# Four attention stages of a two-layer decoder: the order of the score rows, the row maxima and their followers within a batch, and the engine that splits the node biases

## The chip, the cores and the metric

One core of a Trainium2 chip. The time is that of one launch, in microseconds on the device, median of three runs. TensorE multiplies, VectorE (DVE) and ScalarE (ACT) work on tiles and empty PSUM, GpSimd (POOL) works on tiles in SBUF and issues gathers, SyncE (SP) issues the other transfers. The engines run their own instruction streams and meet at semaphores.

## The reference

Four sequences of 256 positions, 128 channels, 16 heads of width 8. Cut to its stages:

```
x = x + L0_attn(layernorm(x))            # kernelised attention (exp features)
x = x + L0_xattn(layernorm(x), ctx)      # softmax attention over ctx, query rows masked
x = x + L0_ffn(layernorm(x))             # three hard-routed trees (q, k, v), attention over
                                         # their outputs, a fourth tree; 255 nodes with bias each
x = x + L1_attn(layernorm(x))            # causal softmax attention
x = x + L1_xattn(layernorm(x), ctx)      # softmax attention over ctx
x = x + L1_ffn(layernorm(x))             # product-key experts, top 16 of 1024 per head

# a softmax attention, per batch and head:
corr = einsum('bhqd,bhkd->bhqk', qh, kh) * scale
prob = softmax(corr, axis=-1)
hidden = einsum('bhqk,bhkd->bhqd', prob, vh)
```

## The kernel before

Work is numbered by n = 4 * stage + batch. n = 0 to 3 is the kernelised attention. The three softmax attentions are in two runs, `RUNS = [(4, 7), (8, 15)]`: batches 4 to 7 are the cross attention of layer 0; then come the trees (`ffn`); batches 8 to 11 are the causal attention and 12 to 15 the cross attention of layer 1; then come the experts (`peer`).

**A batch of a run.** Queries and keys are split into three bf16 parts by GpSimd (`split(n)`), and SP stacks the parts into `stk[n % 3]` with twelve copies of 64 KB (`place(n)`), so that one matmul with a contraction of 51 gives full-precision scores. For each head, `score_rows(n, h)` computes scores with queries on partitions, in two PSUM banks in turn, and VectorE takes each query's maximum (`row_max(n, h)`). When all 16 heads are through, `max_parts(n)` splits the negated maxima into bf16 parts (five instructions), TensorE turns them (`max_turn(n)`), ScalarE copies them out of PSUM (`evac_mt(n)`), and SP copies them into three rows of the stack (`place_max(n)`). Only then can `score_cols(n, h)` compute the scores again with keys on partitions, already less the maximum, in two other banks. ScalarE exponentiates them (`exps(n, h)`), and `values(n, g)` multiplies the probabilities of four heads with the values and a column of ones.

**The followers.** For batch n - 1: `evac_o`, `turn_out` (eight transposes), `onorm` (division by the sums), `tail_a`, `evac_ot`, `tail_b` (output projection), `resid` (VectorE adds it to `x`). For the batches ahead: `norm(n + 3)` with one `power` on GpSimd, `pre_x` (transposes), `evac_x`, `pre_qk`, `evac_qk`, `pre_v`, `evac_v` for n + 2, and its `split` and `place`.

**The order** is written by hand, by head number h, once for each engine, and each engine goes through its list strictly in order. Within batch n, TensorE does `score_cols(n, h)` for h = 0 to 15, and between them the rows of batch n + 1 by

```
ROWS_AT = [[2 * h, 2 * h + 1] if h < 5 else [h + 5] if h < 11 else [] for h in range(H)]
TURN = 13
```

so two heads' rows at each of h = 0 to 4 and one at each of h = 5 to 10. VectorE follows with the maxima, `max_parts(n + 1)` at h = 11 and `norm(n + 3)` at h = 13, `max_turn(n + 1)` is at 13. `pre_x(n + 2)` stands ahead of h = 0. At the start of a run the rows of its first batch run alone.

**The node biases.** The 4 x 255 biases of the trees are split into three bf16 parts on three partitions of `bias_p`, by `split_bias` on VectorE: nine instructions of 255 columns in each of batches 4 to 7, at h = 8. `tree_logits(0)`, behind batch 7, waits for the last (`bias_ready` 3). GpSimd, once the key maximum of stage 0 is reduced over partitions (`kmax_all`), waits in `power(4)` for VectorE's `norm(4)`.

## Time and profile before

| | us |
|---|---|
| median of three runs | 906.93 (904.53 to 907.21) |
| profiled execution, its own time | 905.02 |
| its span, first to last instruction | 903.3 |
| around the span | 1.7 |
| TensorE busy | 704.9 (78%) |
| VectorE busy | 650.5 (72%) |
| ScalarE busy | 443.3 (49%) |
| GpSimd busy | 262.3 (29%) |

The shares are means over stages with different limits. The runs lie from about 123 to 224 us and from 491 to 662 us of the span; the trees stand between them, the experts behind. Times of trace rows are microseconds from the span's start.

### The profile page before, as it was taken

The page shows a single profiled execution, that of the slowest core. Times are in us where ns is not written, and L with a number is a line of the kernel's source. Part 1 is how long each engine was busy: PE and PEld are TensorE (multiplying, and loading weights), DVE is VectorE, ACT ScalarE, POOL GpSimd, SP SyncE. Part 2 cuts the span into 40 slices and gives each one's busy share as a digit, 9 for nine tenths or more (in the row PEclk, how much of TensorE's full clock was granted, in tenths as well). Part 3 has the DMA queues.
Part 4 walks back from the last instruction along what each step waited for, and adds up shares of the span by engine and source line. Part 5 has one row for each costly group of instructions (what it writes and reads, how often), then busy time and mean ns, then how long its engine had stood idle before and what let it go on. Part 6 is the DMA issues. An engine that isn't in the chain of part 4 may idle for free. (4 is left out here: it accounts for less than half of the span.)

```text
span 903.3 us, 15196 instructions
## 1 busy us (share of the span) xinstructions
PE 704.9 (78%) x5016; PEld 529.8 (59%) x5016; DVE 650.5 (72%) x2828; ACT 443.3 (49%) x1051; POOL 262.3 (29%) x242
## 2 busy tenths in 40 slices
PE   3876977878718989888777588887776957878888
PEld 1436524433318777777675366544455956878888
DVE  5665565565559798986596466665538999999984
ACT  1112004345118877888674255555542555565562
POOL 3110221200143232232141121121003027776783
PEclk9886557798958999999888699999997979999999
DMA  8500052200089978898555343322000000000000
GB/s 251 136 1 2 12 64 39 34 6 2 1 308 354 397 275 339 307 397 319 198 194 146 107 54 48 42 38 39 3 1 1 1 1 1 5 4 4 4 8 7
DMA packets 42679, 93.68 MB, mean 104 GB/s; under 512 B 4050, under 2 KB 30194, under 8 KB 34408
## 3 DMA queue, kind: packets, MB, share of 16 engines
q0 software_dynamic: 9216, 69.47, 20.1%
q1 hardware_dynamic: 33384, 23.23, 13.1%
q8 instruction: 40, 0.66, 0.3%
q14 instruction: 39, 0.32, 0.1%
HBM read 74.42 MB, written 0.52 MB: 83 GB/s over the span
## 5 line engine op out<-in xcount | busy, mean ns | idle before, releaser
L742 ACT ACTIVATE arena<-arena,hact 128x128 f32<-128x128 f32 x512 | 155.0, 388 | 1.0
L565 POOL TENSOR_TENSOR arena<-arena 128x1024 f32<-128x1024 f32 x64 | 121.2, 1912 | 82.6 <-DVE arena L1216 65.2
L644 ACT ACTIVATE arena<-psum 128x512 f32<-128x512 f32 (+1 forms) x192 | 102.4, 562 | 81.2 <-PE psum L1366 80.0
L873 DVE TENSOR_REDUCE rowmax<-psum 128x2 f32<-128x512 f32 x128 | 81.5, 686 | 49.6 <-PE psum L1348 48.6
L1067 DVE CUSTOM_DVE_ANT_0 arena<-arena,fx 128x128 f32<-128x128 f32 x384 | 106.0, 344 | 0.3
L1683 PE MATMUL psum<-arena 128*128 128x128 f32 x688 | 86.8, 284 | 21.4 <-DVE arena L1216 19.2
L1572 PE MATMUL psum<-identf,arena 128*128 128x128 f32 x544 | 75.6, 294 | 27.9 <-ACT arena L742 27.3
L1683 PEld LDWEIGHTS psum<-arena 128*128 128x128 f32 x688 | 82.3, 197 | 25.0 <-DVE arena L1216 12.5
L1572 PE MATMUL psum<-arena,identf 128*128 128x128 f32 x544 | 79.5, 304 | 15.3 <-ACT arena L742 14.6
L795 ACT ACTIVATE psum<-arena,tneg 128x1024 f32<-128x1024 f32 x64 | 71.0, 1111 | 39.8 <-POOL arena L565 14.1
L1572 PEld LDWEIGHTS psum<-identf,arena 128*128 128x128 f32 x544 | 68.6, 203 | 35.1 <-ACT arena L742 24.7
L1572 PEld LDWEIGHTS psum<-arena,identf 128*128 128x128 f32 x544 | 72.3, 212 | 22.6 <-issue 16.2
L1348 PE MATMUL psum<-arena 128*128 128x256 bf16 (+1 forms) x384 | 73.7, 291 | 11.9 <-DVE rowmax L873 8.9
L1366 PE MATMUL psum<-arena 128*128 128x256 bf16 (+1 forms) x384 | 70.7, 275 | 12.0 <-DMA arena<-mt 7.5
L587 ACT ACTIVATE arena<-psum 128x128 f32<-128x128 f32 (+3 forms) x66 | 37.9, 577 | 75.5 <-PE psum L1382 18.2
L1216 DVE SCALAR_TENSOR_TENSOR arena<-arena,vaug,psum 128x1024 f32<-128x1024 f32 x43 | 54.3, 1272 | 4.0 <-PE psum L1683 2.3
L1366 PEld LDWEIGHTS psum<-arena 128*128 128x128 bf16 x384 | 32.6, 100 | 37.4 <-ACT arena L644 13.7
L1348 PEld LDWEIGHTS psum<-arena 128*128 128x128 bf16 x384 | 35.3, 104 | 32.7 <-DVE rowmax L873 25.2
L1382 PE MATMUL psum<-arena,vaug 128*32 128x256 f32 (+1 forms) x768 | 51.1, 386 | 1.9 <-ACT arena L644 1.9
L1683 PE MATMUL psum<-arena,picked 128*128 128x128 f32 x336 | 43.2, 283 | 10.5 <-DVE picked L1216 8.2
L473 POOL TENSOR_TENSOR rstd<-var_e,halves 128x2 f32<-128x2 f32 x16 | 11.2, 703 | 136.3 <-DVE var_e L829 136.3
L1683 PEld LDWEIGHTS psum<-arena,picked 128*128 128x128 f32 x336 | 40.2, 196 | 12.3 <-DVE picked L1216 9.8
(215 smaller groups left out, 1235.3 us busy)
## 6 DMA issues: line engine op xcount, KB each, us to landing
arena<-parts SPq DMA_DIRECT2D x144, 64.0 KB
arena<-zeros SPq DMA_DIRECT2D x6, 1232.0 KB
w_sb<-attn_w SPq DMA_DIRECT2D x1, 768.0 KB, 8.1
x<-x_in SPq DMA_DIRECT2D x1, 512.0 KB, 4.4
fx<-ctx_in SPq DMA_DIRECT2D x1, 512.0 KB, 5.4
picked<-mask_in SPq DMA_DIRECT2D x1, 512.0 KB, 6.9
wq_sb<-peer_wq SPq DMA_DIRECT2D x1, 512.0 KB, 7.1
down_sb<-table_down SPq DMA_DIRECT2D x1, 512.0 KB, 7.8
```

The lines of the kernel that those rows point to most:

```text
L565: nc.gpsimd.tensor_tensor(grid[k % 3].rearrange("p (i j) -> p i j", i=PK), sim[:, t, h, :].unsqueeze(2).to_broadcast([P, PK, PK]), sim[:, ...
L644: nc.scalar.activation(probs[k % (2 * HG)][:, 0:w], bank(2 + k % 2, 0, w), ACT.Exp, scale=float(D) ** -0.5).then_inc(probs_ready, 1)
L742: a = nc.scalar.activation(w, w, ACT.Copy, scale=hact[i % 2][:, l:l + 1])
L795: nc.scalar.activation(psum[:, (4 + 2 * (k % 2)) * BANK:(6 + 2 * (k % 2)) * BANK], grid[k % 3], ACT.Exp, bias=tneg[:, t, h:h + 1]).then_in ...
L873: i = nc.vector.tensor_reduce(rowmax[n % 2][:, :, h], bank(k % 2).rearrange("p (s n) -> p s n", s=SUB), AX.X, ALU.max)
L1067: i = nc.vector.tensor_tensor_reduce(w, w, src, 1.0, r[:, LW * E + l:LW * E + l + 1], ALU.mult, ALU.add, hid[g % 4][:, l:l + 1])
L1216: nc.vector.scalar_tensor_tensor(out=picked[k % 3], in0=grid[k % 3], scalar=top[t][:, h, TOPK - 1:TOPK], in1=psum[:, (4 + 2 * (k % 2)) * B ...
L1348: i = nc.tensor.matmul(o[:, r:r + keys], q[:, s * P:s * P + P], kk[:, 0:keys], start=not causal, stop=True, skip_group_check=causal)
L1366: i = nc.tensor.matmul(bank(2 + k % 2, c * S, c * S + S - q0), kk[:, c * P:c * P + P], q[:, q0:S], start=not causal, stop=True, skip_group ...
L1382: i = nc.tensor.matmul(o, vaug[n % 4][:, c, g * HG + j, :], probs[(k + j) % (2 * HG)][:, c * S:c * S + S - q0], start=(c == 0), stop=(c == ...
L1572: i = nc.tensor.matmul(o, *ab, start=(l == 0), stop=(l == LW and f < 3))
L1683: i = nc.tensor.matmul(psum[:, o:o + P], picked[k % 3][:, c * P:c * P + P], diag[t % 2][:, h, :], start=(h == 0 and c % 4 == 0), stop=(h = ...
```

## The change

The rows of a batch are spread by a table of slots. A slot below zero is a head of the batch before: row 0 of batch n + 2 stands at h = 14 of batch n, rows 1 and 2 at h = 15, the other thirteen at h = 0 to 9 of batch n + 1. At the start of a run the three early rows of the second batch follow the first batch's `max_turn`. `max_parts` stands at h = 9 (it was 11), `max_turn` and `evac_mt` at 12 (13), `norm(n + 3)` at 11 (13). `pre_x`, `pre_qk`, `pre_v` stand behind the columns of heads 0, 1, 3 (ahead of head 0, then 0, 1), the `values` groups at 6, 11, 13 and at head 2 of the next batch (5, 9, 13, 1), `turn_out` and `tail_a` at 4 and 7 (3, 6), with ScalarE's and VectorE's lists to match. `norm(6)` moves behind the first batch's `max_parts`, and GpSimd's `split(5)` ahead of `power(6)`. The node biases are split by GpSimd, all 1020 columns at once, ahead of `power(4)`, in a tile of their own.

```diff
-        nbias_sb, nbias_w = arena2[0:3, 4096:5116], arena2[0:3, 3072:3072 + 510].bitcast(bf16)
+        nbias_sb, nbias_w = arena2[0:3, 4096:5116], sb("nbias_w", [3, 4 * NODES], bf16)[:, :]
...
-        ROWS_AT = [[2 * h, 2 * h + 1] if h < 5 else [h + 5] if h < 11 else [] for h in range(H)]
-        TURN = 13
+        ROW_SLOTS = [-2, -1, -1, 0, 1, 1, 2, 2, 3, 4, 4, 6, 6, 7, 8, 9]
+        EARLY = len([i for i in ROW_SLOTS if i < 0])
+
+        def rows_at(n, h, last):
+
+            return ([(n + 1, j) for j in range(H) if ROW_SLOTS[j] == h and n + 1 <= last]
+                    + [(n + 2, j) for j in range(H) if ROW_SLOTS[j] == h - H and n + 2 <= last])
...
             pool.wait_ge(kmax_all, 1)
+            pool.wait_ge(in_tab, 32)
+            p = bias_p[:, 9 * P:NB]
+            for j in range(3):
+                row = identf[0:3, j:j + 1].to_broadcast([3, 4 * NODES])
+                link(nc.gpsimd.tensor_copy(nbias_w, nbias_sb))
+                if j < 2:
+                    link(nc.gpsimd.tensor_tensor(nbias_sb, nbias_sb, nbias_w, ALU.subtract))
+                link(nc.gpsimd.tensor_tensor(nbias_w if j else p, nbias_w, row, ALU.mult))
+                if j:
+                    link(nc.gpsimd.tensor_tensor(p, p, nbias_w, ALU.add))
+            nc.gpsimd.tensor_copy(nbias_w[:, 0:1], p[:, 0:1]).then_inc(nbias_ready, 1)
             power(B)
             power(B + 1)
             split(B)
+            split(B + 1)
             power(B + 2)
-            split(B + 1)
...
# ScalarE, in run()
-                    if n + 2 <= last:
-                        evac_x(n + 2)
                     for h in range(H):
                         exps(n, h)
-                        if n > first and h == 1:
-                            evac_o(n - 1)
-                        if n + 2 <= last and h == 0:
-                            evac_qk(n + 2)
-                        if n + 2 <= last and h == 1:
-                            evac_v(n + 2)
-                        if h == TURN and n + 1 <= last:
+                        if n + 2 <= last:
+                            if h == 0:
+                                evac_x(n + 2)
+                            elif h == 1:
+                                evac_qk(n + 2)
+                            elif h == 3:
+                                evac_v(n + 2)
+                        if n > first:
+                            if h == 2:
+                                evac_o(n - 1)
+                            elif h == 7:
+                                evac_ot(n - 1)
+                        if h == 12 and n + 1 <= last:
                             evac_mt(n + 1)
-                        if h == 8 and n > first:
-                            evac_ot(n - 1)
...
# VectorE
-            norm(B + 2)
             def run(first, last):
                 for h in range(H):
                     row_max(first, h)
                 max_parts(first)
+                if first == B:
+                    norm(B + 2)
+                for h in range(EARLY):
+                    row_max(first + 1, h)
                 for n in range(first, last + 1):
                     for h in range(H):
-                        if n + 1 <= last:
-                            for hh in ROWS_AT[h]:
-                                row_max(n + 1, hh)
-                        if n > first and h == 5:
-                            onorm(n - 1)
-                        if n > first and h == 11:
-                            resid(n - 1)
-                        if n + 1 <= last and h == TURN - 2:
+                        for m, hh in rows_at(n, h, last):
+                            row_max(m, hh)
+                        if n > first:
+                            if h == 4:
+                                onorm(n - 1)
+                            elif h == 9:
+                                resid(n - 1)
+                        if h == 9 and n + 1 <= last:
                             max_parts(n + 1)
-                        if h == 13 and n + 3 <= last:
+                        if h == 11 and n + 3 <= last:
                             norm(n + 3)
-                        if h == 8 and first == B:
...
-                            split_bias(nc.vector, link, j, j + NODES)
...
# TensorE
                 max_turn(first)
+                for h in range(EARLY):
+                    score_rows(first + 1, h)
                 for n in range(first, last + 1):
-                    if n + 2 <= last:
-                        pre_x(n + 2)
                     for h in range(H):
                         score_cols(n, h)
+                        for m, hh in rows_at(n, h, last):
+                            score_rows(m, hh)
+                        if n + 2 <= last:
+                            if h == 0:
+                                pre_x(n + 2)
+                            elif h == 1:
+                                pre_qk(n + 2)
+                            elif h == 3:
+                                pre_v(n + 2)
+                        if n > first:
+                            if h == 2:
+                                values(n - 1, 3)
+                            elif h == 4:
+                                turn_out(n - 1)
+                            elif h == 7:
+                                tail_a(n - 1)
+                            elif h == 9:
+                                tail_b(n - 1)
+                        if h == 6:
+                            values(n, 0)
+                        elif h == 11:
+                            values(n, 1)
+                        elif h == 13:
+                            values(n, 2)
+                        if h == 12 and n + 1 <= last:
+                            max_turn(n + 1)
...
-                    pe.wait_ge(bias_ready, 3)
+                    pe.wait_ge(nbias_ready, 1)
```

## Rows read from the trace of the kernel before

**Rows 1.** Busy time by stretch: batches 4, 5, 7, 8, 11, 14, 15.

```profile
core 0: us, PE busy (x) PEld busy (x) DVE busy (x) ACT busy (x) POOL busy (x), PEclk, DMA share, GB/s
...
139.60:163.80 24.20, 19.79 (x129) 9.99 (x130) 15.58 (x37) 10.34 (x19) 4.94 (x6) 0.78 0.27 35
163.80:190.40 26.60, 21.61 (x159) 11.86 (x158) 15.10 (x35) 11.67 (x22) 4.25 (x5) 0.85 0.24 32
...
213.70:224.30 10.60, 9.56 (x85) 4.78 (x86) 4.03 (x14) 6.96 (x13) 0.00 (x0) 0.88 0.01 2
...
511.80:531.20 19.40, 17.16 (x157) 11.77 (x158) 11.99 (x44) 9.09 (x20) 4.23 (x5) 0.87 0.34 44
...
571.30:591.30 20.00, 16.64 (x170) 11.11 (x170) 13.93 (x33) 10.27 (x23) 4.22 (x5) 1.00 0.33 43
...
632.00:652.30 20.30, 15.88 (x147) 8.71 (x148) 12.11 (x26) 10.47 (x19) 0.00 (x0) 1.00 0.01 3
652.30:661.70 9.40, 8.37 (x85) 4.67 (x86) 1.01 (x4) 6.62 (x12) 0.00 (x0) 1.00 0.00 0
```

**Rows 2.** Timeline of batch 11: start, us, engine, line, [idle before].

```profile
572.06 0.60 PE L1247 MATMUL psum<-xn_t,w_sb 128*128 128x256 f32 x2
...
575.23 1.02 ACT L587 ACTIVATE arena<-psum 128x1024 f32<-128x1024 f32 x1 [1.12 <-PE psum L1382]
...
575.30 0.60 PE L1348 MATMUL psum<-arena 128*128 128x256 bf16 x4
...
575.72 2.48 DVE L873 TENSOR_REDUCE rowmax<-psum 128x2 f32<-128x512 f32 x4 [0.81 <-PE psum L1348]
...
576.47 0.39 PE L1348 MATMUL psum<-arena 128*128 128x256 bf16 x2 [0.29 <-DVE rowmax L873]
...
577.30 1.05 PE L1306 MATMUL psum<-identf,arena 128*128 128x128 f32 x8
...
585.65 2.01 ACT L644 ACTIVATE arena<-psum 128x384 f32<-128x384 f32 x4 [1.46 <-PE psum L1366]
...
588.14 0.86 PE L1382 MATMUL psum<-arena,vaug 128*32 128x256 f32 x16
```

**Rows 3.** The same timeline at the end of batch 11.

```profile
586.48 0.41 DVE L862 TENSOR_TENSOR x<-psum,x 128x256 f32<-128x256 f32 x1
...
587.91 0.29 PE L1394 MATMUL psum<-identb,mparts 128*48 128x128 bf16 x2 [0.78 <-DVE mparts L887]
...
588.25 0.38 ACT L587 ACTIVATE mt<-psum 48x256 bf16<-48x256 bf16 x1 [0.58 <-PE psum L1394]
...
590.69 0.44 PE L1263 MATMUL psum<-identf,xn 128*128 128x128 f32 x2 [1.04 <-DVE xn L834]
...
591.33 0.39 PE L1366 MATMUL psum<-arena 128*128 128x256 bf16 x2 [0.21 <-DMA arena<-mt]
```

**Rows 4.** SP's timeline: the twelve copies of `place`, batches 9 and 13.

```profile
496.41 12.48 SPq L409 DMA_DIRECT2D arena<-parts  x12
...
574.42 7.91 SPq L409 DMA_DIRECT2D arena<-parts  x12
```

**Rows 5.** VectorE's timeline: a node split of 255 biases, first and last of nine.

```profile
181.12 0.27 DVE L261 CAST arena<-arena 3x255 bf16<-3x255 f32 x1
...
184.10 0.28 DVE L271 TENSOR_TENSOR bias_p<-bias_p,arena 3x255 bf16<-3x255 bf16 x1
```

**Rows 6.** GpSimd: its wait for `norm(4)`, and two lines (min/median/max ns).

```profile
100.54 0.74 POOL L473 TENSOR_TENSOR rstd<-var_e,halves 128x2 f32<-128x2 f32 x1 [23.33 <-DVE var_e L829]
```

```profile
L495 POOL TENSOR_TENSOR resid_f<-qk_f,parts x12: 1151/1156/1161, 108.7 to 614.3; 128x512 f32<-128x512 f32 x12
```

```profile
L565 POOL TENSOR_TENSOR arena<-arena x64: 1905/1911/1957, 685.5 to 887.5; 128x1024 f32<-128x1024 f32 x64
```

**Rows 7.** Timelines of VectorE and GpSimd: the first `key_features`; `norm(6)` beside `split(5)`.

```profile
78.61 0.69 DVE L940 TENSOR_SCALAR arena<-arena 128x1024 f32<-128x1024 f32 x1 [1.22 <-ACT arena L664]
...
122.47 1.41 DVE L834 TENSOR_SCALAR xn<-x,mv,rstd 128x128 f32<-128x128 f32 x2 [0.87 <-POOL rstd L473]
```

```profile
122.39 0.72 POOL L491 TENSOR_TENSOR qk_f<-qk_f,maskrow 128x256 f32<-128x256 f32 x1
```

More of the change, by code:

```diff
@@ L206, in decoder_program @@
         out_done = sem("out_done")
+        nbias_ready = sem("nbias_ready")
         bias_ready, osb_ready, or_ps = sem("bias_ready"), sem("osb_ready"), sem("or_ps")
@@ L254, in split_bias @@
         def split_bias(engine, link, a, b):
-            p = bias_p[:, a:b]
-            if a < 9 * P:
-                src, w = bias_sb[:, a:b], bias_w[:, a:b]
-            else:
-                src, w = nbias_sb[:, a - 9 * P:b - 9 * P], nbias_w[:, a - 9 * P:b - 9 * P]
+            p, src, w = bias_p[:, a:b], bias_sb[:, a:b], bias_w[:, a:b]
             link(engine.tensor_copy(w, src))
@@ L973, in run @@
                 max_parts(first)
+                if first == B:
+                    norm(B + 2)
+                for h in range(EARLY):
+                    row_max(first + 1, h)
                 for n in range(first, last + 1):
                     for h in range(H):
-                        if n + 1 <= last:
-                            for hh in ROWS_AT[h]:
-                                row_max(n + 1, hh)
-                        if n > first and h == 5:
-                            onorm(n - 1)
-                        if n > first and h == 11:
-                            resid(n - 1)
-                        if n + 1 <= last and h == TURN - 2:
+                        for m, hh in rows_at(n, h, last):
[6 more added lines that the diff above has]
+                        if h == 9 and n + 1 <= last:
                             max_parts(n + 1)
-                        if h == 13 and n + 3 <= last:
+                        if h == 11 and n + 3 <= last:
                             norm(n + 3)
-                        if h == 8 and first == B:
-                            if n == first:
-                                dve.wait_ge(in_tab, 32)
-                            j = 9 * P + (n - first) * NODES
-                            split_bias(nc.vector, link, j, j + NODES)
-                            if n == last:
-                                nc.vector.tensor_copy(nbias_w[:, 0:1], bias_p[:, j:j + 1]).then_inc(bias_ready, 1)
                 if first == B:
@@ L1485, in run @@
                 max_turn(first)
+                for h in range(EARLY):
+                    score_rows(first + 1, h)
                 for n in range(first, last + 1):
-                    if n + 2 <= last:
-                        pre_x(n + 2)
                     for h in range(H):
                         score_cols(n, h)
-                        if n + 1 <= last:
-                            for hh in ROWS_AT[h]:
-                                score_rows(n + 1, hh)
-                            if h == TURN:
-                                max_turn(n + 1)
-                        if n + 2 <= last and h == 1:
-                            pre_v(n + 2)
-                        if h % HG == 1:
-                            if h > HG:
-                                values(n, h // HG - 1)
-                            elif n > first:
-                                values(n - 1, HG - 1)
-                        if n + 2 <= last and h == 0:
-                            pre_qk(n + 2)
-                        if n > first and h == 3:
-                            turn_out(n - 1)
-                        if n > first and h == 6:
-                            tail_a(n - 1)
-                        if n > first and h == 9:
-                            tail_b(n - 1)
```

## The prediction

> **What bounds the kernel now.** I read first the busy time and granted clock of stretches cut at the first key-major score of each batch (`score_cols(n, 0)`, here C0) [rows 1]. Seven batches of the second run repeat at 19.4 to 20.7 us; from 531.2 to 632.0 five take 100.8 us. In a batch of 20.0 us TensorE is busy for 16.6, VectorE 13.9, ScalarE 10.3, GpSimd 4.2: no engine is full. The first run does the same work and takes 24.2, 26.6 and 23.3 us (190.4 to 213.7). A stretch that fills no engine is set by a chain of waits, so I read the timeline of one batch for each engine's beat [rows 2] and for the end of the batch [rows 3].
>
> The beats at 2.4 GHz: a pair of score matmuls, rows (R) or columns (C), takes TensorE 0.22 us when it waits for nothing (four matmuls issued in 0.44). The row maximum starts 0.42 after its R (575.30, 575.72), the maxima follow at 0.60, and the R into the same bank may go 0.75 after that start (576.47). Exponentials run at 0.50 us each (0.54 for 512 columns). `turn_out` takes 0.9 us, a `values` 0.8 (1.0 where both halves are full), the four matmuls of `pre_qk` 0.87, `evac_o` 0.92 until the next can start [rows 2].
>
> The end of a batch: residual at 586.48, `max_turn` 1.43 later at 587.91, the maxima leave PSUM at 588.25, their copy by DMA lets C0 start at 591.33, 3.08 later. This copy ends the batch; the norm of n + 3 (2.8 us, from the end of the maxima to the transposes of `pre_x` at 590.69) stands behind the maxima, too, and lets TensorE wait 1.04 [rows 3]. So the period is the time from C0 to `evac_mt` plus 3.06. As a test of these beats I laid out the present order by hand, head by head: row 15 is issued at 14.2 after C0, maxima finished 16.7, `evac_mt` 17.0, next C0 at 20.06. The trace has 20.0.
>
> **The change, part by part.** *Order of the runs.* I lay out the new order with the same beats, C0 = 0, for a batch with all followers. R3 0.4 (it waits for the maxima of rows 0 to 2, just made), `pre_x` 0.6, C1 0.9, R4 and R5 1.2 and 1.6, `pre_qk` 1.8 to 2.7 (0.87 for its four matmuls), C2 2.7, R6 and R7 2.9 and 3.1, `values` of the last group to 4.3, C3, R8, `pre_v` to 5.3, C4, R9 and R10 5.5 and 5.75. `turn_out` waits for `evac_v`, which stands on ScalarE behind the 0.92 us `evac_o` and an exponential: 6.4 to 7.3, a stall of 0.45. C5, C6, R11, R12 7.3 to 7.9, `values` to 9.15, C7, R13 9.4, `tail_a`, C8, R14 10.0, C9, R15 10.5, `tail_b` from 10.75 to 11.35 (11.6 with a bias). VectorE adds the residual at 11.7 to 11.9 and `max_turn` can go 1.43 later, 13.1 to 13.3; `evac_mt` follows exponential 12 at 13.8. Next C0 not before 13.8 + 3.06 = 16.9.
>
> What else can hold that C0: the norm of n + 3 occupies VectorE from 13.1 to 15.85, so row maximum 0 of n + 2 starts at 15.85, R2 may go at 16.6 and ends at 16.8: level with the DMA. The rows of n + 2 need their 12 copies: SP issues them from some 4.1 (after `pre_qk`, ScalarE and the first GpSimd cast), 7.9 us of issuing [rows 4], to 12.0, landed by 14.2 at the lag of the maxima's copy; R0 comes at 14.7. SP then is free for `place_max` at 13.9. Period 17.0, gain 3.15 for each of the five: 15.8. The batch before the last has nobody two ahead: 16.3 by the same layout against 20.3, gain 4.0. In the last one `tail_b` no longer stands behind the `values` of head 9; its residual comes 8.25 after C0 instead of 9.4: 1.2. The run's first batch: its maxima wait for DMA until 511.85 in any case, the three rows taken ahead now sit in front of C0 at 1.2 GHz (1.1 lost), and lay-out gives the next C0 at 530.2 for 531.2: 1.0. Second run: 15.8 + 4.0 + 1.2 + 1.0 = 22.0.
>
> *First run.* Here VectorE also loses the node split: nine instructions, 181.12 to 184.38, 3.3 us in each of four batches [rows 5], and in three of them ahead of the maxima, on the chain just named. That and a clock of 0.78 to 0.85 [rows 1] are what its batches have above 20. New batch 4: it starts at 1.2 GHz as before, where its projections with bias take 2.8 and 2.0 us: laid out, 21.2 against 24.2, gain 3.0. Batch 5: 17.4 with biases, plus 1.0 allowed for a slow start, 18.4 against 26.6: 8.2. Batch 6: 16.7 against 23.3: 6.6. Batch 7 to its residual: 8.8 against 10.6: 1.8. Sum 19.6. Before C0 of batch 4 I count 0: the norm that leaves the way of the row maxima was mostly covered by the wait for ones, and R2 of batch 5, behind the norm, fills the wait for the maxima's copy (bounds -1 to +1).
>
> *Behind each run* the leaf and expert stages start from the last-but-one residual through the norms on VectorE (8.9 us, while the last `values` end 6 us after that residual), so they shift by the whole gain.
>
> *Node biases on GpSimd.* Eleven instructions over 1020 columns in place of 36 on VectorE over 255, queued ahead of `power(B)`. A 128x512 `tensor_tensor` with one bf16 input takes 1.156 us, one of 1024 columns 1.911 [rows 6]: 2.3 each for 1020 as the upper price; ten at 2.3 make 23.0, and if the three casts, which read one input, cost half of it, 19.6; with gaps 20.5 (the eleventh writes one column). The engine idles 23.3 us up to 100.54, from 77.2 [rows 6]: covered, by 2.8. If three partitions or a broadcast input made them twice as dear, 41 us, `power(B)` and all behind it would come 18 late. `tree_logits`, which waits for the result, is 130 us later.
>
> *What the chain does to VectorE.* The one `tensor_scalar` that ran beside a GpSimd instruction of 0.72 us took, two of them, 1.41 instead of 0.60 [rows 7]. The first `key_features` (78.61, 0.69 us), for which TensorE waits, falls into the first subtract of the new chain (about 78.6 to 80.9). Bounds 0 and 2.3 (one whole instruction); I take 2.2, the row being such a case. The other three have 2 us and more of slack, and they push the chain back by their own 2.8 at most, while `power(B)` itself moves by 2.2. The Trainium skill (SBUF — State Buffer, "Who interferes with whom") says such a pair locks the shared ports for a whole instruction, either way round; by it the sum holds the full 2.3, and the trace agrees with 0.81 lost beside 0.72.
>
> *The earlier `split(B+1)`* brings the copies of batch 5 some 4 us forward; they weren't waited for.
>
> **Sum.** 22.0 + 19.6 - 2.2 = 39.4. The profiled execution took 905.0 (903.3 span, 1.7 around it), so 865.6; its runs have a median 1.9 higher, so I say 866.
>
> **Rivals.** *Rows of n + 2 come late.* They stand at heads 14 and 15, in TensorE's queue ahead of the next C0, and have 0.5 us of slack at R0 and none at R2. For it: SP took 12.48 us for twelve copies at 496.41 [rows 4]; against: in the steady batches it took 7.9. At 1.04 each they land at 18.2 and the period is 19.6; over ten batches 26 us are lost, 892. A slip of 1.5 us a batch, from this or from waits that my layout rounds away, gives 866 + 15 = 881. Chance 0.20.
>
> *GpSimd's chain overruns* the idle stretch, twice the price: 866 + 18 = 884. Against it: the 1024-column row has two broadcast inputs and costs no more than its columns. 0.08.
>
> *The clock (the slower side).* In the first run its mean is 0.78, 0.85 and 0.88 in batches 4, 5 and 7; in the second, with waits of 0.78 and 1.04 at each batch's end, it holds 1.00 [rows 1, 3]. The new order has waits of 1.2 us at R2 and, ahead of the last batch, 2. If every batch began with 8 us at 1.2 GHz, that is 4 us a batch, ten batches 40: 906, no gain; from there on it is slower, and with whole batches at 1.2 GHz (15 us of TensorE work doubled) 12 us each: 866 + 120 = 986. TensorE's busy share rises instead, so 0.05. The Trainium skill (TensorE: Matmul & The Clock Gate, "HAM oscillation") has idle stretches between bursts send the clock back, which would put this kernel on that side; the second run's rows speak against it for waits this short.
>
> **Chances.** Forecast 0.62, with 857 to 875 as its own range (2 us on each run's start, 4 on the first run's clock, 0.5 a batch on the layout). With most of the late-rows case the range 857 to 887 holds 0.8. A measurement of this kernel tells about 0.3%, 2.7 us. Faster: 0.62 + 0.20 + 0.08 + 0.02 for odd cases = 0.92; same 0.03; slower 0.05.
>
> **What would show it.** C0 to C0 of 17.0 in the second run; the wait before C0 on the maxima's copy or R2's bank, under 0.5 us; `turn_out` waiting 0.45 behind `evac_v`; norm no longer ahead of `pre_x`; clock 1.00 from batch 5 on; GpSimd busy for 20 us from 77.2, and the first `key_features` late by 2. It would be wrong if R0 waited for the stacked parts, if `evac_mt` came later than 14 us after C0, or if `power(B)` started over 3 us later than now.

## The result, and the profile after it

The changed kernel takes 889.57 us (median of 4 runs, 888.94 to 889.86) against 906.06 (904.53 to 907.21) for the kernel before on the same chip: ratio 0.9824, 95% interval 0.9809 to 0.9840. It is faster, by 16.5 us, where 40 were forecast, and it lies outside the range of 857 to 887. The profiled span is 887.7 us.

Busy time by batch, cut at the first key-major score (C0) of each batch as in [rows 1]; batches 4, 5, 7, 8, 9, 10, 11, 12, 14 and 15:

```profile
core 0: us, PE busy (x) PEld busy (x) DVE busy (x) ACT busy (x) POOL busy (x), PEclk, DMA share, GB/s
141.60:161.90 20.30, 15.49 (x123) 8.51 (x122) 11.72 (x27) 9.85 (x19) 4.95 (x6) 0.92 0.32 42
161.90:181.90 20.00, 18.77 (x162) 11.15 (x160) 12.57 (x26) 11.42 (x22) 4.27 (x5) 0.93 0.29 43
...
199.90:208.50 8.60, 7.20 (x68) 4.18 (x68) 1.01 (x4) 6.62 (x12) 0.00 (x0) 1.00 0.01 2
499.60:519.00 19.40, 15.02 (x149) 10.76 (x148) 10.92 (x40) 8.46 (x19) 4.22 (x5) 0.85 0.34 44
519.00:539.50 20.50, 18.03 (x187) 13.72 (x186) 13.24 (x49) 10.00 (x22) 4.23 (x5) 0.90 0.32 42
539.50:558.10 18.60, 17.77 (x189) 13.40 (x187) 13.17 (x49) 10.00 (x22) 4.24 (x5) 0.91 0.24 46
558.10:577.30 19.20, 15.79 (x172) 11.12 (x170) 14.18 (x34) 9.91 (x22) 4.23 (x5) 1.00 0.35 46
577.30:597.20 19.90, 16.88 (x157) 10.76 (x155) 14.28 (x33) 11.39 (x22) 4.23 (x5) 0.91 0.33 43
...
617.30:635.90 18.60, 16.36 (x149) 9.07 (x147) 12.46 (x26) 10.83 (x20) 0.00 (x0) 0.91 0.01 2
635.90:644.20 8.30, 6.90 (x67) 4.02 (x67) 1.01 (x4) 6.53 (x12) 0.00 (x0) 1.00 0.01 2
```

The first run's batches fell from 24.2 and 26.6 us [rows 1] to 20.3 and 20.0, about as forecast. The full batches of the second run, 9 to 14, are 18.6 to 20.5 us where 17.0 was forecast (16.3 for batch 14), and the granted clock, 1.00 in the rows of batches 11 and 14 before, is 0.90 to 0.92 in most. The same in five stretches, cut at `power(4)`, the last residual of the first run, `evac_mt(8)`, the last residual of the second run and the end of the span (us; each is a difference of two starts in a timeline of one profiled execution; the last four rows are experiments told below):

| | to `power(4)` | first run | between | second run | rest |
|---|---|---|---|---|---|
| before | 100.5 | 123.8 | 279.3 | 158.1 | 241.6 |
| changed | 102.7 | 106.0 | 280.8 | 155.2 | 243.1 |
| node split alone | 102.6 | 112.4 | 281.5 | 159.5 | 242.6 |
| order alone | 98.0 | 111.8 | 280.7 | 158.5 | 243.0 |
| half the copies | 102.6 | 106.1 | 283.7 | 144.8 | 241.7 |
| best version | 100.3 | 106.6 | 282.8 | 137.9 | 243.0 |

The change gains 17.8 us in the first run and 2.9 in the second, and loses 2.2 at the start and 1.5 in each of the other stretches. Two cautions go with the table. The first column holds the first stage too, whose end varies from profile to profile: GpSimd's reduction comes at 76.5 us before, 76.1 in the changed kernel and 73.8 in the order alone, and from there to `power(4)` it is 24.0, 26.6 and 24.2 us. And in the second run "changed" and "order alone" have the same instruction lists, and still take 155.2 and 158.5 us, so that of the 2.9 us gained there no part is certain. The second run, with 22.0 us forecast, is the miss. Its waits, from TensorE's and SP's timelines of batch 11:

```profile
563.53 7.91 SPq L411 DMA_DIRECT2D arena<-parts  x12
...
577.07 0.39 PE L1359 MATMUL psum<-arena 128*128 128x256 bf16 x2 [2.67 <-DMA arena<-parts]
...
577.41 0.33 PE L1377 MATMUL psum<-arena 128*128 128x256 bf16 x2
```

The first row scores of batch 13 (L1359) wait 2.67 us for the stacked parts, and the next C0 (L1377) stands behind them in TensorE's queue. Such a wait stands ahead of the C0 of each of batches 8 to 14: 8.21, 4.13, 2.36, 0.49, 2.67, 2.40 and 1.49 us. (The first run has two, of 4.04 and 1.23 us, ahead of the C0 of batches 5 and 6.) C0 of batch 15 has no rows ahead of it and waits 1.47 for the maxima's copy. What the copies do meanwhile is in the DMA share, for the same train and for one of the kernel before (issued from 534.37 to 542.3):

```profile
563.50:565.50 2.00, 1.98 (x24) 1.37 (x16) 1.44 (x3) 1.66 (x4) 1.78 (x4) 1.00 0.12 33
565.50:567.50 2.00, 1.77 (x17) 1.72 (x18) 1.69 (x5) 0.80 (x4) 1.15 (x1) 1.00 0.52 87
...
573.50:575.50 2.00, 0.90 (x19) 0.38 (x11) 0.87 (x4) 0.75 (x2) 0.70 (x1) 1.00 0.62 64
575.50:577.50 2.00, 0.43 (x4) 0.40 (x5) 0.00 (x0) 0.00 (x0) 0.00 (x0) 1.00 0.12 14
577.50:579.50 2.00, 1.80 (x11) 1.04 (x10) 1.82 (x3) 0.60 (x2) 0.00 (x0) 0.54 0.02 4
```

```profile
542.40:544.40 2.00, 2.00 (x32) 1.47 (x29) 1.66 (x6) 1.64 (x4) 0.00 (x0) 1.00 0.63 74
544.40:546.40 2.00, 1.97 (x28) 1.45 (x16) 0.64 (x3) 0.73 (x2) 0.00 (x0) 1.00 0.63 69
546.40:548.40 2.00, 1.18 (x16) 0.56 (x17) 1.76 (x10) 1.43 (x4) 0.00 (x0) 1.00 0.00 0
```

The last column but one is the DMA share. SP is done issuing 7.9 us after the first copy (at 571.4), yet the engines go on at a share of 0.62 until about 576: the train takes 12 to 12.5 us from first issue to last byte, and R0 follows 13.5 us after the first issue. The kernel before shows the same 12 us; there nobody waited. The last row of the first fence shows the price of the wait: the granted clock falls to 0.54. The Trainium skill (Perfetto Trace Analysis, "What 'DMA-bound' means") says that the profiled window of the issuing sequencer is descriptor generation and not data movement; these rows agree, 7.9 against some 12 us.

A late row also delays the batch behind it. Behind the R0 at 577.07 shown above come:

```profile
577.30 0.27 PE L1373 MATMUL psum<-causal_k,identb 128*128 128x256 bf16 x1
...
578.32 0.61 PE L1359 MATMUL psum<-arena 128*128 128x256 bf16 x2 [0.20 <-DVE rowmax L888]
...
579.58 0.63 PE L1274 MATMUL psum<-identf,xn 128*128 128x128 f32 x2
```

C0 of batch 12 starts at 577.30. R2 waits for the maxima of R0 and comes 1.0 us behind C0 instead of ahead of it, and `pre_x` (L1274) 2.3 us behind, where the layout has 0.6. So the next train starts late as well, 5.5 to 6.8 us after C0 in batches 9 to 13, and `evac_mt` comes 14.9 to 17.0 us after C0 in batches 9 to 14, where 4.1 and 13.8 were laid out.

GpSimd's part, its timeline and a DMA window around the start of its chain:

```profile
76.14 0.70 POOL L515 PARTITION_ALL_REDUCE kmaxg<-kmax  x1 [15.33 <-DVE kmax L946]
76.90 1.02 POOL L577 CAST nbias_w<-arena 3x1020 bf16<-3x1020 f32 x1
85.44 2.12 POOL L579 TENSOR_TENSOR arena<-arena,nbias_w 3x1020 f32<-3x1020 f32 x1 [7.52 <-issue]
...
102.56 0.18 POOL L583 COPY nbias_w<-bias_p 3x1 bf16<-3x1 bf16 x1
102.70 0.73 POOL L475 TENSOR_TENSOR rstd<-var_e,halves 128x2 f32<-128x2 f32 x1
```

```profile
q14 instruction: 1, 0.01, 1.2%
```

The chain takes 1.1 us for its first cast and 17.3 (85.4 to 102.7) for the rest, 18.4 where 20.5 was priced. But between its first and its second instruction lie 7.5 us in which GpSimd waits for nothing that the profile shows. In 77 to 79 us one packet of instructions comes in on queue 14. It does not mark such a gap: the kernel before has one in 100 to 102 us, where `power(4)` starts without a gap, and the run with seven operations ahead, told below, has a gap of 6.8 us (82.9 to 89.7) without one. The first `key_features` (78.24, 0.69 us) falls into the gap and isn't delayed.

### The profile page after: what moved, and what is told of

Read it like the earlier page. It is cut to its first block and busy times, and to the rows that moved or that the text cites. A ratio compares the mean times of both kernels' runs of the same rounds, so it can differ in the third digit from the quotient of the medians.

```text
span 887.7 us, 15168 instructions
## 1 busy us (share of the span) xinstructions
PE 700.2 (79%) x5016; PEld 533.6 (60%) x5016; DVE 640.8 (72%) x2791; ACT 440.9 (50%) x1051; POOL 280.0 (32%) x253
## 3 DMA queue, kind: packets, MB, share of 16 engines
q0 software_dynamic: 9216, 69.47, 20.5%
## 5 line engine op out<-in xcount | busy, mean ns | idle before, releaser
L657 ACT ACTIVATE arena<-psum 128x512 f32<-128x512 f32 (+1 forms) x192 | 102.8, 561 | 86.5 <-PE psum L1377 85.4
L1078 DVE CUSTOM_DVE_ANT_0 arena<-arena,fx 128x128 f32<-128x128 f32 x384 | 106.0, 350 | 0.3
L1700 PE MATMUL psum<-arena 128*128 128x128 f32 x688 | 87.3, 285 | 21.3 <-DVE arena L1227 19.2
L1700 PEld LDWEIGHTS psum<-arena 128*128 128x128 f32 x688 | 82.8, 199 | 24.5 <-DVE arena L1227 12.9
L1359 PE MATMUL psum<-arena 128*128 128x256 bf16 (+1 forms) x384 | 79.4, 307 | 22.6 <-DMA arena<-parts 12.3
L1589 PE MATMUL psum<-arena,identf 128*128 128x128 f32 x544 | 78.6, 299 | 15.4 <-ACT arena L757 14.6
L1589 PEld LDWEIGHTS psum<-arena,identf 128*128 128x128 f32 x544 | 70.5, 206 | 23.5 <-issue 16.2
L1377 PE MATMUL psum<-arena 128*128 128x256 bf16 (+1 forms) x384 | 70.3, 278 | 4.6 <-DMA arena<-mt 2.9
L1359 PEld LDWEIGHTS psum<-arena 128*128 128x128 bf16 x384 | 36.4, 108 | 45.4 <-DVE rowmax L888 22.9
L1377 PEld LDWEIGHTS psum<-arena 128*128 128x128 bf16 x384 | 34.4, 102 | 26.4 <-ACT arena L657 14.7
L1393 PE MATMUL psum<-arena,vaug 128*32 128x256 f32 (+1 forms) x768 | 48.0, 367 | 1.9 <-ACT arena L657 1.9
L1700 PEld LDWEIGHTS psum<-arena,picked 128*128 128x128 f32 x336 | 40.5, 197 | 11.3 <-DVE picked L1227 8.9
L1078 DVE DVE_READ_ACCUMULATOR2_ANT hid<- 128x1 f32 x512 | 43.3, 84 | 0.0
```

The lines of the kernel that those rows point to most:

```text
L657: nc.scalar.activation(probs[k % (2 * HG)][:, 0:w], bank(2 + k % 2, 0, w), ACT.Exp, scale=float(D) ** -0.5).then_inc(probs_ready, 1)
L1078: i = nc.vector.tensor_tensor_reduce(w, w, src, 1.0, r[:, LW * E + l:LW * E + l + 1], ALU.mult, ALU.add, hid[g % 4][:, l:l + 1])
L1359: i = nc.tensor.matmul(o[:, r:r + keys], q[:, s * P:s * P + P], kk[:, 0:keys], start=not causal, stop=True, skip_group_check=causal)
L1377: i = nc.tensor.matmul(bank(2 + k % 2, c * S, c * S + S - q0), kk[:, c * P:c * P + P], q[:, q0:S], start=not causal, stop=True, skip_group ...
L1393: i = nc.tensor.matmul(o, vaug[n % 4][:, c, g * HG + j, :], probs[(k + j) % (2 * HG)][:, c * S:c * S + S - q0], start=(c == 0), stop=(c == ...
L1589: i = nc.tensor.matmul(o, *ab, start=(l == 0), stop=(l == LW and f < 3))
```

## The experiments

Each ratio is to the kernel before on the same chip, with its 95% interval; it can differ from the quotient of two medians by up to 0.3%.

**Half the copies.** From batch 11 on only terms 0 to 2 of six are copied, so that the scores use stale rows for the rest.

```diff
-                    for r, term in enumerate(TERMS):
+                    for r, term in enumerate(TERMS if n < 11 else TERMS[:3]):
```

> The changed kernel, but from batch 11 on only six of the twelve stacked copies are made (the rows of the other terms keep old data), so their transfer takes about half as long. If the late rows are the cause (the twelve copies end 13.5 us after their first issue and row 0 of n + 2 waits for them), the waits before that row vanish in batches 9 to 13 and these take 17.0 to 17.5 us instead of 20.5, 18.6, 19.2, 19.9 and 20.1, batch 14 about 16.5 instead of 18.6: about 14 us less, 875. If the layout of the forecast was wrong by itself (the new order costs its 19.7 us a batch through VectorE, ScalarE and the bank waits), the time stays within 3 us of 889.6.

0.9689 (0.9642 to 0.9736), 879.1 us. From the first short train on, no row waits for parts, and `evac_mt` to `evac_mt` takes 17.0, 16.8, 17.3, 17.8 and 16.6 us; clock 1.00. The order gives what the layout said, 17.0, once the copies are in time: in batches 10 to 14 the first copy is issued 4.1 to 4.2 us after C0 and `evac_mt` comes after 13.5 to 14.7. From `evac_mt(10)` to `evac_mt(15)` it is 85.5 us against 101.0 before.

**No early rows.** Rows 0 to 3 of batch n + 1 are all issued behind C0 of batch n.

```diff
-        ROW_SLOTS = [-2, -1, -1, 0, 1, 1, 2, 2, 3, 4, 4, 6, 6, 7, 8, 9]
+        ROW_SLOTS = [0, 0, 0, 0, 1, 1, 2, 2, 3, 4, 4, 6, 6, 7, 8, 9]
```

> The changed kernel with rows 0 to 2 back behind the columns of head 0 of their own predecessor batch (slots 0, 0, 0, 0, 1, ...). Late rows: row 0 now comes 2 to 3 us later and in front of it nothing waits at heads 14 and 15, the copies are still a train of 13.5 us from about 4 us after C0, so batches of about 18 us, 883 to 887, and a clock of 1.00. Order at fault: four rows at head 0 push everything by two row maxima (1.2 us a batch), 895 or more.

0.9920 (0.9894 to 0.9947), 898.2 us: slower than the change, and where the second forecast, an order at fault, had put it (895 or more). The profile doesn't tell the two apart so simply: its first run takes 110.8 us (106.0 in the change), its second 157.7 (155.2). In the second TensorE now waits for the maxima's copy ahead of C0, by 4.95 us at 521.20:

```profile
506.65 7.91 SPq L411 DMA_DIRECT2D arena<-parts  x12
514.99 0.77 SPq L417 DMA_DIRECT2D arena<-mt  x1
```

```profile
521.20 0.40 PE L1373 MATMUL psum<-causal_k,identb 128*128 128x256 bf16 x1 [4.95 <-DMA arena<-mt]
```

That copy is queued on SP behind the train: `evac_mt` at 514.60 is followed by C0 6.6 us later, where [rows 3] have 3.08, and 3.1 to 4.8 us later in batches 10 to 14. Where it is clearly more than 3.1, C0 comes 13.8 to 14.6 us after the train's first issue. So the train's end binds C0 even if no row waits for it, which the layout had not counted either. How much of the loss the four rows at head 0 make by themselves, 1.2 us a batch by the forecast, is not separated.

**Two queues.** GpSimd issues the six copies of parts 1 and 2 that it has just written, SP the other six.

```diff
+                for part in (1, 2):
+                    ...
+                                nc.gpsimd.dma_start(stk[n % 3][r * D:(r + 1) * D, :, w, :],
+                                                    parts[n % 2][:, part, w, :]).then_inc(stkp_ready[n % 3], 16)
```

> The changed kernel with the six copies of parts 1 and 2 issued by GpSimd behind its split, those of part 0 still by SP. If what paces the train is one queue, two queues end it 4 us earlier, row 0 of n + 2 waits no more and the time falls to about 877. If it is the way each copy lands (64 KB into eight partitions), the end stays at 13.5 us after the first issue and the time at 888 to 892; GpSimd's issuing may even make power(n + 3) later.

0.9781 (0.9726 to 0.9835), 885.2 us, between the two forecasts; its interval overlaps that of the change. The two queues issue side by side and the DMA share rises to between 0.84 and 1.07 in the middle of a train, and the last bytes move some 11 us after the first issue. But where R0 waits it still follows 12.9 to 14.1 us after the first issue, 13.3 to 13.7 with one queue (the train of batch 12, for a reason not looked into, is shorter with either: 11.9 and 11.7):

```profile
515.29 0.37 PE L1374 MATMUL psum<-causal_q,identb 128*128 128x256 bf16 x1 [3.63 <-issue]
```

This is R0(10); the profile names no releaser, but R0 waits here for nothing but the copies of the two queues. The gain lies elsewhere: from `evac_mt(8)` to `evac_mt(9)` it is 17.1 us for 23.5, and the rest of the run takes 131.0 for 131.7. The first train of the second run stands on SP behind other copies and is issued at 1.06 us a copy (12.75 for twelve, from 481.71, in the changed kernel); that is what the second queue seems to relieve, though part of the 6.4 us is only moved, since `evac_mt(8)` itself comes 1.5 us later behind the first run. In the steady batches one queue isn't the cause.

**Half the bytes.** Twelve copies, each of half the columns; the scores use stale values in the other half.

```diff
-                                sp.dma_start(stk[n % 3][r * D:(r + 1) * D, :, w, :],
-                                             parts[n % 2][:, part, w, :]).then_inc(...)
+                                c = S if n < 11 else S // 2
+                                sp.dma_start(stk[n % 3][r * D:(r + 1) * D, :, w, 0:c],
+                                             parts[n % 2][:, part, w, 0:c]).then_inc(...)
```

> From batch 11 on each of the twelve copies of stacked parts moves only the first half of its columns (128 pieces of 256 bytes in place of 128 of 512 bytes); the second halves keep what an earlier batch left. If the bytes set the train's length, it falls from 13.5 to about 7 us, as with six whole copies, and the time comes near to 879 (ratio 0.970). If the number of pieces or of copies sets it, the train stays at 12 to 13.5 us, the waits for it stay, and so does the time: ratio 0.980 to 0.984. I hold the second for the likelier (0.65), as the engines show a busy share of 0.63 at only 58 GB/s.

0.9686 (0.9648 to 0.9724), 877.0 us, the same as with half the copies. I had held the other outcome for likelier; it fell. `evac_mt` to `evac_mt` is 16.6 to 17.8 us in batches 10 to 14. The train, by windows of 2 us from its first issue at 562.25:

```profile
564.30:566.30 2.00, 1.85 (x18) 1.72 (x18) 1.69 (x5) 0.80 (x3) 1.07 (x1) 1.00 0.23 52
...
570.30:572.30 2.00, 1.97 (x32) 1.05 (x28) 1.73 (x9) 1.43 (x5) 0.00 (x0) 1.00 0.14 32
572.30:574.30 2.00, 1.53 (x24) 0.94 (x14) 1.05 (x5) 1.17 (x3) 0.70 (x1) 1.00 0.04 12
```

The share is 0.23 in place of 0.63, and the copies end with the issuing. So a whole copy (128 pieces of 512 bytes into 8 partitions) is paced by its bytes and not by the number of pieces or copies, some 0.95 us each against 0.66 of issuing; a half one by SP.

**Projections where they were.** `pre_x(n + 2)` back ahead of head 0, `pre_qk` at head 0, `pre_v` at head 1, on TensorE and ScalarE.

```diff
+                    if n + 2 <= last:
+                        pre_x(n + 2)
                     for h in range(H):
                         ...
                             if h == 0:
-                                pre_x(n + 2)
-                            elif h == 1:
                                 pre_qk(n + 2)
-                            elif h == 3:
+                            elif h == 1:
                                 pre_v(n + 2)
```

> The changed order of rows, but the projections of batch n+2 where the kernel before has them (transposes of x ahead of head 0, queries and keys at head 0, values at head 1). Theory T1 (the train of twelve copies ends some 13.5 us after its first issue, and the first score rows of n+2 wait for it; in the changed kernel the first copy goes out 5.4 to 6.7 us after a batch's first columns): the train starts some 2.5 to 3 us earlier in a batch, the waits of the first rows for the stacked parts (2.4, 2.4 and 1.5 us in the last three trains) vanish or fall under 0.5 us, and the eight batches of the second run become 17.5 to 18.5 us instead of 18.3 to 20.5: 875 to 881 us. Rival T2 (the changed places of the projections were needed, to keep them out of the way of the first columns and of the last group of values): the batches stay at 19 to 20 us and the time at 887 to 892. Forecast 878, ratio to the kernel before 0.970.

0.9743 (0.9710 to 0.9776), 881.2 us. The trains start earlier (3.1 to 4.6 us after C0 in batches 8 to 12, for 5.4 to 6.8), the last waits fall from 2.67, 2.40 and 1.49 to 1.43, 1.38 and 0.55, and the second run takes 148.5 us. The direction and most of the size are T1's; the waits didn't vanish, since C0 comes earlier too and R0 still follows a first issue after 13.3 to 13.7 us.

**Each half alone.** The node split on GpSimd in the kernel before, and the new order with VectorE splitting at head 8.

```diff
 before.py, GpSimd (the 36 instructions on VectorE are gone):
+            for j in range(3):
+                link(nc.gpsimd.tensor_copy(nbias_w, nbias_sb))
+                ...
             power(B)
 after.py, VectorE (GpSimd's chain is gone):
+                        if h == 8 and first == B:
+                            ...
+                            split_bias(nc.vector, link, j, j + NODES)
```

> The kernel before with the node split alone moved to GpSimd. If VectorE's nine instructions stood on the chain to the maxima in batches 4 to 6, this gives 3 x 3.3 back, less 2.0 for the late power(4): 898. If they were covered, only the 2.0 is left: 908.

> The changed order of rows alone, with the node biases split by VectorE at head 8 of the batches of the first run, as in the kernel before. The other half alone, e4, gave 0.987, of about 0.9824 for both. T1 (the split's 3 us of VectorE stand ahead of the maxima, which end a batch's score rows, so both orders lose about as much by it): order alone keeps what the second run gives, 4.9 us, and half or more of the first run's: ratio 0.990 to 0.993. Rival T2 (the new order, with its maxima at head 9, hides the split under other work): ratio 0.984 to 0.987.

Split alone 0.9870 (0.9828 to 0.9912), near its first forecast; order alone 0.9880 (0.9842 to 0.9918), between its two. The ratios gain 1.30% and 1.20%, and 1.76% together: they don't add. By the table the split alone takes 11.4 us from the first run and the order alone 12.0, both together 17.8, not 23.4: that both take work off the same chain, from the rows of a batch to its maxima, is the reading of this, and no run takes it apart further. The profile of the split alone is the slowest of its five executions, 5.3 us above their median, so its row may be too long somewhere. In the second run neither gains (159.5 and 158.5 for 158.1); in the order alone it starts with a wait of 9.99 us for the train of batch 9.

**GpSimd's gap.** First, seven operations of the chain ahead of the reduction, three and the last copy behind it; then only three ahead, held back until VectorE works out of PSUM; then these three with the early projections.

```diff
+            pool.wait_ge(in_tab, 32)
+            pool.wait_ge(dd_ps, B)
+            part_of(0)
             pool.wait_ge(kmax_ready, 1)
             nc.gpsimd.partition_all_reduce(kmaxg[:, :], kmax1[:, :], P, RMAX).then_inc(kmax_all, 1)
```

> GpSimd's chain for the node biases is cut in two: its first seven operations ahead of the wait for the key maxima (GpSimd idles there for 15.3 us), the other three and the last copy behind the reduction over the partitions. T1 (the 7.5 us of idling between the chain's first and second operation belongs to what follows the reduction, whatever operation it is, such as new code being loaded): the gap stays behind the reduction, now ahead of the third part's operations, the chain ends near 90 us, power(4) is back at 100.5 us and the first run starts 2.0 to 2.2 us earlier: 887.5 less about 2, ratio to the kernel before 0.979 to 0.981. Rival T2 (the gap belongs to the first tensor_tensor of the chain): it moves ahead of the reduction, which is then delayed by some 2 us or more, and nothing is gained or 2 us are lost: ratio 0.982 to 0.985. Rival T3: new code is wanted in both directions, and the reduction is late by up to 7 us: ratio 0.985 to 0.99.

> The changed kernel, with only the first three operations of GpSimd's chain for the node biases (5.2 us) ahead of the reduction over the partitions, and held back there until TensorE's last features of the first stage (the moment from which VectorE works out of PSUM: 68.5 us in the changed kernel's profile), so that they do not run beside VectorE's small operations of the bias split, which took up to ten times as long beside them in the run before this one. T1 (7.5 us of loading behind the reduction, and operations that share a port with VectorE's): the three operations end near 74, the reduction stays at 76.1 to 76.5 us, the chain ends near 97.5, power(4) is at 100.5 and everything after it is 2 us earlier: ratio 0.9795 to 0.9805. Rival T2: VectorE's work out of PSUM is slowed too, or the reduction waits for code of its own: it comes at 78 us or later and nothing is gained (0.982 to 0.986).

> The early projections of e5 with the cut chain of e9. The two act at different places, so their gains should add: e5's 878.7 less 2.1, so 876.5 to 878.5, ratio 0.972.

Seven ahead: 0.9884 (0.9847 to 0.9921), slower than the change. Three ahead: 0.9855 (0.9820 to 0.9890); with the projections 0.9736 (0.9700 to 0.9771), the same as without. Lines of the two, first VectorE and GpSimd with seven ahead, then GpSimd with three:

```profile
61.49 1.84 DVE L258 CAST arena<-arena 3x128 bf16<-3x128 f32 x1
...
70.61 2.14 DVE L261 TENSOR_TENSOR arena<-arena 3x128 f32<-3x128 f32 x1
```

```profile
89.70 1.88 POOL L525 TENSOR_TENSOR nbias_w<-nbias_w,identf 3x1020 bf16<-3x1020 bf16 x1 [6.76 <-issue]
...
104.43 0.74 POOL L475 TENSOR_TENSOR rstd<-var_e,halves 128x2 f32<-128x2 f32 x1 [10.42 <-DVE var_e L845]
```

```profile
78.77 0.38 POOL L527 PARTITION_ALL_REDUCE kmaxg<-kmax  x1 [5.69 <-issue]
...
86.98 2.11 POOL L520 TENSOR_TENSOR arena<-arena,nbias_w 3x1020 f32<-3x1020 f32 x1 [6.74 <-issue]
```

The gap stays behind the reduction and in front of the first operation with two tensors, whichever it is; and once such operations come shortly ahead of the reduction, it waits 5.7 us as well, and so do the key maxima's users. (With seven ahead that wait doesn't show: 8.7 us lie there in any case, until VectorE's key maxima are ready.) Beside GpSimd's chain VectorE's small operations of the bias split take 1.84 and 2.14 us for 0.20 and 0.28, which with seven ahead made the key maxima 5 us late. Neither way gains the 2 us. The Trainium skill (GPSIMD Engine Reference, "2.1 Instruction dispatch") says that the first call of a freshly loaded kernel pays a load of about 6 us that no instruction in the profile shows; the gaps of 5.5 to 7.6 us agree with it in size. The page speaks of the first call; here they come at each such change within one launch, also in front of operations used before. No row shows what is loaded, so that code is the cause stays a reading.

**The best version.** Early projections and two queues, first with three operations ahead of the reduction, then with the chain where the change has it but its last addition and copy behind `power(4)`.

```diff
             power(B)
+            link(nc.gpsimd.tensor_tensor(p, p, nbias_w, ALU.add))
+            nc.gpsimd.tensor_copy(nbias_w[:, 0:1], p[:, 0:1]).then_inc(nbias_ready, 1)
             power(B + 1)
```

> e10, and the six copies of parts 1 and 2 issued by GpSimd, as in e3. T1 (the bytes of the copies set the train's length, 768 KB in some 13.5 us, but two queues overlap a little: 12 to 12.5 us in e3): the waits of the first rows, 1.4, 1.4 and 0.5 us in the last trains of e5, vanish: 873 to 876. Rival T2 (GpSimd's own issues of 1.1 us each come ahead of its power and split, and delay the projections of a later batch): 877 to 882.

> The early projections of e5 and the two queues of e3, GpSimd's chain for the node biases behind the reduction as in the changed kernel, but with its last addition and the last copy (2.1 and 0.2 us) behind power(4), in the 5 us in which GpSimd waits for the next variances. In e9 to e11 the three operations ahead of the reduction let it wait 5.5 us for code of its own, so nothing was gained there. T1: power(4) comes 24.5 to 24.8 us after the reduction in place of 26.6 (the changed kernel) and the start of the first run is 2 us earlier than there; the rest as in e11, whose start came 26.0 to 26.7 us behind the key maxima: ratio 0.966 to 0.967. Rival T2: the addition shares VectorE's port just when VectorE scales x for batch 4, and gives back most of it: ratio 0.968.

0.9682 (0.9646 to 0.9717), 875.3 us, and 0.9639 (0.9609 to 0.9669), 871.8 us. In both the waits for parts are short but not gone: R0 waits 2.89, 0.95, 0.83 and 0.88 us at 510.81, 530.24, 565.14 and 582.80 in the second one (no releaser named, as above), 12.8 to 13.4 us after the first issue. Two windows of that one, cut at `evac_mt` of batches 11, 12 and 13:

```profile
545.90:562.90 17.00, 15.80 (x171) 11.14 (x170) 13.90 (x33) 9.87 (x24) 7.76 (x11) 1.00 0.45 50
562.90:580.60 17.70, 15.92 (x163) 10.04 (x165) 14.11 (x35) 11.11 (x24) 7.76 (x11) 1.00 0.45 49
```

Here a batch of 17.0 us stands in a kernel that computes everything; the batches from 10 to 14 take 17.9, 17.0, 17.7, 18.4 and 16.7. Of the 17.3 us that the second run gains on the change, 6.6 lie between `evac_mt(8)` and `evac_mt(9)`, against 2.0 lost ahead of it. Two VectorE lines, of this kernel and of the change, show what sharing costs:

```profile
101.10 2.38 DVE L869 TENSOR_SCALAR xn<-x,mv,rstd 128x128 f32<-128x128 f32 x2 [0.92 <-POOL rstd L478]
```

```profile
103.47 0.60 DVE L849 TENSOR_SCALAR xn<-x,mv,rstd 128x128 f32<-128x128 f32 x2 [3.12 <-POOL rstd L475]
```

`power(4)` is early again (100.32), but the scaling of x beside GpSimd's addition takes 2.38 us for 0.60, so that it ends only 0.6 us before that of the change, and 1.8 of the 2.4 us are given back, as T2 had it. The ratio is below the forecast of either theory, but its interval reaches T1's; the intervals of the two versions overlap, so that this edit's own worth isn't settled.

## Why the prediction was wrong where it was

- **The end of a batch and the period.** Right as long as no row is late. The sum C0 to `evac_mt` plus 3.06 gave 17.0; the runs with half of the copies and with half of the bytes show 16.6 to 17.8, the best version, with waits of up to 0.95 us, 16.7 to 18.4. The 3.06 is no fixed lag: in the change C0(11) comes 2.07 after its `evac_mt`. And the sign named in advance, `evac_mt` later than 14 us after C0, came in the change (14.9 to 17.0): late rows make late maxima.
- **The step that failed** is "landed by 14.2 at the lag of the maxima's copy; R0 comes at 14.7". I took the end of issuing and added the lag of a lone copy. In the trace R0 comes 13.5 us after the first issue, not 10.6. That is the error; the 4.1 until the first issue was right where no row is late (4.1 to 4.2 with half the copies). But a late R0 pushes R2, `pre_x` and the next train back, so that in batch 11 the first of the twelve is issued 5.46 us after C0 (558.07): 19.0 in place of 14.7. The queue holds the maxima's copy, too, behind the train, which I had free at 13.9. Had I read the DMA share of one train of the kernel before, it would have said so: 0.63 until 12 us after the first issue. With 5.46 + 13.5 = 19.0 for R0 and C0 0.2 behind it, the batch takes the 19.2 us measured.
- **The rival "rows of n + 2 come late"** (0.20) was the case that came true, by a slip of some 2 us a batch in the second run; its reason, slow issuing of 1.04 us a copy, was not the cause in the steady batches. Issuing stayed at 0.66; the transfer is what takes 0.95. The first train of the second run was issued as slowly as feared (1.06 a copy). The rival's own sum has a slip: 4.1 + 12.5 of issuing and the same 2.2 of lag make 18.8, not 18.2.
- **The run's first batch** was to gain 1.0. It gained nothing (19.4 us as before), and the three early rows put the train of batch 9, issued slowly until 494.5, ahead of C0(8): 8.21 us of waiting, C0 10.2 us after `evac_mt(8)` in place of 8.2.
- **First run.** Right within 2 us: 19.6 forecast, 17.8 measured (3.9, 6.6, 5.3 and 2.0 by batch for 3.0, 8.2, 6.6 and 1.8). Partly luck: two waits for trains, 5.3 us together, weren't in the sum, and batch 4 still came out 0.9 shorter than laid out. The two halves of the change overlap there by 5.6 us.
- **GpSimd's chain.** The loss at the start was right in size, 2.2, by luck, and wrong in cause. The chain costs less than priced (18.4 us for 20.5), but the 7.5 us behind the reduction take up all its cover. Sharing with VectorE, which I had blamed, did not touch the first `key_features`; it shows where operations do meet (1.33 us for 0.69 at 89.83, and the lines above).
- **The clock.** Behind the waits for parts it falls to 0.50 to 0.54, as the rival said of waits, after 1.49 us at 617 as well as after 2.67; but over the second run it is 0.89 (0.96 before), not so low that the gain is lost. With waits under 1 us it is 1.00 from `evac_mt(10)` to `evac_mt(15)` of the best version.
- **Still open.** The unchanged work between the runs and behind them takes 1.5 us more each. The granted clock is 0.77 for 0.93 in the first 26 us behind the first run, but other kernels here vary by as much without a pattern (0.64 with half the copies, 0.93 with two queues). Why 155.2 and 158.5 us come of the same order in the second run isn't known; 2.5 us of it lie in the first batch (23.5 and 26.0 us from `evac_mt(8)` to `evac_mt(9)`). Nor is it known why two queues end the bytes about 1 us sooner and bring R0 only some 0.6 sooner.

## What to carry to other kernels

- A train of copies has not landed before the DMA share falls; the end of its issuing plus the lag of a lone copy says nothing of it. Before an order makes work wait for a train of copies, read the windows of DMA share over one of today's trains, even where nobody waits for it.
- Two edits that shorten the same chain may not add (11.4 and 12.0 us alone, 17.8 together): run each alone before the sum is believed.
- Not all of an engine's idle stretch need be cover for new work: here a two-tensor operation behind a reduction over partitions came 6.7 to 7.6 us late, and nothing of this showed where 23.3 us of waiting lay between the two.

## What the runs showed of the hardware that was not expected

- Twelve copies of 64 KB from 128 partitions into 8 each take some 11.3 us to move at a share of 0.63 of the DMA engines, issued from one queue, and the first row that needs them all follows 13.3 to 13.7 us after the first issue; from two queues the share reaches 1.2 in windows of 2 us (the profile adds up the times of packets, which can overlap) and the bytes end about 1 us sooner, but that row still follows after 12.8 to 14.1; with 32 KB each the share is 0.23.
- A copy of 24 KB queued behind such a train lands behind it: C0, which waits for it, came 6.6 us after `evac_mt` in place of 3.1.
- GpSimd idles 6.7 to 7.6 us between `partition_all_reduce` and the next operation with two tensors (a cast in between runs at once), and 5.5 to 5.7 us between such an operation and the reduction.
- Over three partitions of 1020 columns GpSimd takes 1.02 us for a cast and 1.88 to 2.44 for an operation with two inputs (1.37 and 2.62 at most, in other runs).
- VectorE's operations out of SBUF beside GpSimd's take up to GpSimd's own time: 1.84 us for 0.20; reductions out of PSUM beside them stay at 1.2 (with three operations ahead, 67.9 to 71.7 us).
